# Splits, rotation tables and first block of the attention layer made beside the local stage

## What is computed

```python
x = x + layernorm(sparse_attention(layernorm(x)))    # compressed + selected + window branches, gated
x = x + layernorm(ffn_part(layernorm(x)))            # two layers of _layer below
```

```python
starts = np.arange(0, Lp - W + 1, W // 2)            # W = 64
win = xw[:, starts[:, None] + np.arange(W)]
win_out = attend(win, Wq, bq, Wk, bk, Wv, bv)        # softmax(q k^T * SCALE) v
out = concat([comp_out * g0, sel_out * g1, win_out * g2]) @ Wo + bo
out = out * 0.5 + hidden_states * 0.5
return (out - out.mean(-1)) * rsqrt(out.var(-1) + 1e-06)
```

```python
h = shift_token(x)                  # second half of the columns from the token before
q, k, v = split(h @ wqkv)
q = l2norm(q) * qs ; k = l2norm(k) * ksc
q, k = rotary_xpos(q, k)            # cos/sin tables times a scale by position
x = x + local_attention(q, k, v) @ wo
h = layernorm(shift_token(x)) * lg + lb
a, g = split(h @ w1 + b1)
x = x + (a * gelu(g)) @ w2 + b2
```

## Time and profile before

| | us |
|---|---|
| median of 3 runs (lowest, highest) | 1570.95 (1570.84, 1571.41) |
| the profiled execution's own time | 1571.91 |
| its span, first to last instruction | 1570.0 |
| TensorE / VectorE / ScalarE / GpSimd busy | 1468.3 / 1167.7 / 1033.9 / 779.5 |
| mean granted TensorE clock, share of 2.4 GHz | 0.972 |

### The profile page before, as it was taken

The page is one execution under the profiler, slowest core; times in us unless marked ns, Lnnn a source line. Parts: engine busy times, 40 slices in busy tenths (PEclk is TensorE's granted clock), DMA queues, the critical chain, the costliest instruction groups (busy, mean ns, idle before and its releaser), DMA issues.

```text
span 1570.0 us, 35727 instructions
## 1 busy us (share of the span) xinstructions
PE 1468.3 (94%) x10355; PEld 1214.9 (77%) x10355; DVE 1167.7 (74%) x3324; ACT 1033.9 (66%) x2610; POOL 779.5 (50%) x966
## 2 busy tenths in 40 slices
PE   8899992799999999988999979999999999799996
PEld 6468881688888888867888868888888887688885
DVE  6762686788888888876556568888888887666664
ACT  5222575588888888874545448888888888455553
POOL 4003245566666666633222536666666665344442
PEclk9999996899999999999999999999999999899998
DMA  5002233100000000002000020000000000000101
GB/s 179 1 1 69 95 101 90 55 7 6 6 5 5 5 5 5 5 8 83 14 13 9 14 65 5 7 6 5 5 5 5 5 5 6 31 28 28 53 28 54
DMA packets 57521, 44.04 MB, mean 28 GB/s; under 512 B 13214, under 2 KB 55386, under 8 KB 57442
## 3 DMA queue, kind: packets, MB, share of 16 engines
q1 hardware_dynamic: 57442, 43.07, 9.0%
HBM read 26.24 MB, written 8.39 MB: 22 GB/s over the span
## 4 chain that ended last, share of the span: by engine, by line
PE 80%; DVE 9%; ACT 4%; issue 4%; POOL 3%; DVEq 1%; ACTq 0%; DMA 0%; POOLq 0%; SPq 0%; PEldq 0%
PE bank L1948 7%; PE bank L1916 7%; PE bank L1862 7%; PE bank L1875 7%; PE bank L1781 6%; PE bank L1783 6%; PE bank L1782 6%; PE bank L1809 4%; PE bank L2019 4%; PE bank L2021 4%; PE bank L2020 4%; PE bank L1643 2%; PE bank L1703 2%; PE bank L1705 2%; PE bank L1704 2%
## 5 line engine op out<-in xcount | busy, mean ns | idle before, releaser
L1232 ACT ACTIVATE prob<-prob,neg_max 128x256 f32<-128x256 f32 x512 | 257.8, 507 | 9.2 <-DVE neg_max L2549 5.9
L798 POOL TENSOR_TENSOR rnorm<-sumsq,neg_half 128x8 f32<-128x8 f32 x128 | 213.0, 1664 | 23.4 <-POOL sumsq L795 23.4
L812 POOL TENSOR_TENSOR qk_cos<-qk_cos,qk_sin 128x512 f32<-128x512 f32 x128 | 181.1, 1415 | 60.7 <-DVE qk_cos L2413 44.9
L1781 PE MATMUL bank<-wqkv_hi,hT_hi 128*128 128x512 f32 x384 | 176.1, 458 | 4.9 <-DVE hT_lo L2399 4.9
L2019 PE MATMUL bank<-h_hi,w_hi 128*128 128x512 f32 (+1 forms) x352 | 143.7, 408 | 12.5 <-POOL h_lo L860 12.5
L1783 PE MATMUL bank<-wqkv_hi,hT_lo 128*128 128x512 f32 x384 | 154.8, 403 | 0.0
L1782 PE MATMUL bank<-wqkv_lo,hT_hi 128*128 128x512 f32 x384 | 153.9, 401 | 0.0
L1374 ACT ACTIVATE act_hi<-act_full 128x512 fp32r<-128x512 f32 x96 | 60.7, 632 | 138.9 <-DVE act_full L2735 137.4
L1916 PE MATMUL bank<-ident,prob 128*128 128x128 f32 x1024 | 147.1, 276 | 3.0 <-DVE prob L2588 2.1
L1916 PEld LDWEIGHTS bank<-ident,prob 128*128 128x128 f32 x1024 | 117.9, 141 | 30.4 <-DVE prob L2588 3.4
L2020 PE MATMUL bank<-h_hi,w_lo 128*128 128x512 f32 (+1 forms) x352 | 141.0, 401 | 0.0
(11 more groups left out here) (278 smaller groups left out, 4062.1 us busy)
## 6 DMA issues: line engine op xcount, KB each, us to landing
x_sb<-in_L_attn_hidden_states SPq DMA_DIRECT2D x8, 512.0 KB, 7.1
x_in<-in_L_attn_hidden_states SPq DMA_DIRECT2D x8, 512.0 KB, 4.8
x_scratch<-x_in SPq DMA_DIRECT2D x8, 512.0 KB, 3.0
f_x<-x_scratch SPq DMA_DIRECT2D x8, 512.0 KB, 4.1
out<-f_y SPq DMA_DIRECT2D x8, 512.0 KB, 3.0
raw<-in_L_ffn_w SPq DMA_DIRECT2D x6, 640.0 KB
hs<-x_sb SPq DMA_DIRECT2D x16, 224.0 KB
hs<-x_sb SPq DMA_DIRECT2D x64, 56.0 KB
```

The source lines that it names most:

```text
L798: pool.tensor_tensor(rnorm[:, part * HEADS:(part + 1) * HEADS], sumsq[:, which * HEADS:(which + 1) * HEADS], neg_half[:, 0:HEADS], ALU.pow ...
L812: pool.tensor_tensor(qk_cos[:, which], qk_cos[:, which], qk_sin[:, which], ALU.add).then_inc(z_ready[which], 1)
L1232: act.activation(prob[:, h], prob[:, h], ACT.Exp, bias=neg_max[:, h:h + 1], scale=-1.0, accum_out=psums[:, h:h + 1]).then_inc(exped, 1)
L1781: pe.matmul(bank[:, to], hT_hi[:, c], wqkv_hi[:, c, cols], start=(c == 0), stop=False)
```

## The change

The SBUF layout is made anew: rope, wqkv_hi, wqkv_lo, sc_x and wo_sb now start above everything that the local stage uses, while w1, w2, h_in and prob take the place of xnT and its weights; qTw and vw go over qT_lo and kT_lo. hT_hi and hT_lo still lie over the x_in ring (slot 0). The second and third rendezvous are gone. Work that stood between them is put into the local stage:

- ScalarE makes wqkv_hi in four halves (128x768) at the ends of its iterations n = 8, 11, 14, 17; VectorE wqkv_lo at the ends of its iterations 10, 13, 16, 19.
- GpSimd makes the scales after group step G = 1 and all eight tables, one at the end of each step G = 1 to 8.
- GpSimd stages block 0 at the start of G = 8; TensorE transposes it before its last window output; ScalarE makes hT_hi at n = 44, between `norm_x1` of group 6 and of group 7; VectorE makes hT_lo after its loop.
- `clear` comes after ScalarE's step 0 of layer 0.
- SP waits for the previous group's moves and store before issuing the next; GpSimd waits for the moves of groups 0 and 1, and after six steps for all.

```diff
+TABLES = 6 + 8
+SPLIT_AT = (8, 11, 14, 17)
+QKV_HALVES = (slice(0, 3 * INNER // 2), slice(3 * INNER // 2, 3 * INNER))
...
             def move_group(g):
                 sp.wait_ge(x_made, GB * (g + 1))
+                if g:
+                    sp.wait_ge(hs_moved, 48 * g)
+                    settle(sp)
...
-            await_phase(sp, 2)
             for lay in range(DEPTH):
-                if not lay:
-                    end_phase(sp, 3)
...
+            def stage_first():
+                pool.wait_ge(win_qk_ps, NB)
+                pool.wait_ge(hs_moved, 48)
+                settle(pool)
+                pool.tensor_copy(h_in[:, 0], x_sb[:, 0, 0:P]).then_inc(h_staged, 1)
+                pool.tensor_copy(h_in[:, 1], hs[:, 0, :]).then_inc(h_staged, 1)
             for G in range(1, NG + 3):
+                if G == NG:
+                    stage_first()
                 if 0 <= G - 2 < NG - LATE:
                     make_x1(G - 2)
                 if G - 1 < NG:
                     sum_scales(G - 1)
                 if 0 <= G - 3 < NG:
                     x1_scales(G - 3)
-            arrive(pool)
-            await_phase(pool, 2)
+                if G == 1:
+                    scales(0)
+                if G <= 8:
+                    table(*tables()[G - 1]).then_inc(sc_made, 1)
+            pool.wait_ge(hs_moved, 48 * 2)
...
+            def first_hi():
+                act.wait_ge(hT_ps, 1)
+                act.wait_ge(x1_stored, 16 * 5)
+                act.activation(hT_hi[:], bank[:, 3, 0:2 * P]..., ACT.Copy).then_inc(hT_hi_ready, 1)
...
+                if n == NB + 12:
+                    first_hi()
                 if r < 2 and 0 <= n - 16 < NB:
                     norm_x1(b)
                     norm_x1(b + 1)
-            end_phase(act, 2)
-            for c in range(DC):
-                act.activation(wqkv_hi[:, c], raw[:, c], ACT.Copy).then_inc(split_hi, 1)
+                if n in SPLIT_AT:
+                    c, h = divmod(SPLIT_AT.index(n), 2)
+                    act.wait_ge(raw_attn, 16)
+                    act.activation(wqkv_hi[:, c, QKV_HALVES[h]], raw[:, c, QKV_HALVES[h]], ACT.Copy).then_inc(split_hi, 1)
...
+                if n == NB - 1:
+                    first_turn()
                 win_out(n)
-            end_phase(pe, 2)
...
-            dve.wait_ge(x_made, NB)
-            await_phase(dve, 2)
+                lo(0, ahead=True)
+                if lay: ...
+                else:
+                    dve.wait_ge(x_made, NB)
+                    dve.wait_ge(x1_stored, 16 * NG)
```

More of the change, by code:

```diff
@@ L92, in build @@
         place("spare", [P, 2 * P])
+        sin_at = base[0]
+        sin_raw = place("sin_raw", [P, 2, BPB * 32])
         ident = place("ident", [P, P])
@@ L136, in build @@
         pT = place("pT", [P, 2, 4 * P])
-        oT = place("oT", [P, INNER // P, P])
         bst = place("bst", [P, GB, 2, 6])
@@ L204, in build @@
         pTw = place("pTw", [P, 2, P])
-        base[0] = after_const
+        base[0] = rope_at
+        wv_sb = place("wv_sb", [P, DC, D])
+        wc_sb = place("wc_sb", [P, RATIO * DC, D])
+        wo3_sb = place("wo3_sb", [P, 3 * DC, D])
+        wsg_sb = place("wsg_sb", [P, DC, 32])
+        bo_bc = place("bo_bc", [P, D])
+        iota1 = place("iota1", [P, P])
         l_bst = place("l_bst", [P, NB, 6])
@@ L921, in _ @@
                     scales(lay + 1)
-                    for a in range(2):
-                        for i in range(2):
-                            for h in range(2):
-                                table(a, i, h).then_inc(sc_made, 1)
+                    for which in tables():
+                        table(*which).then_inc(sc_made, 1)
                     pool.wait_ge(hs_moved, moved_in(lay + 1) - 48)
@@ L1124, in _ @@
                     act.wait_ge(x1_stored, 16 * NG)
-                    clear()
-                    end_phase(act, 3)
                 k0 = lay * NB
                 def hi(b):
+                    if not lay and type(b) is int and b == 0:
+                        return
                     act.wait_ge(hT_ps, k0 + b + 1)
@@ L1676, in win_out, with first_turn @@
                 pe.matmul(bank[:, 6 + j % 2, 0:D], pTw[0:WK, j % 2], vw[0:WK, j % 2], start=True, stop=True).then_inc(win_o, 1)
+            def first_turn():
+                pe.wait_ge(h_staged, 2)
+                pe.wait_ge(win_v, NB)
+                for c in range(DC):
+                    tr = pe.transpose(bank[:, 3, c * P:(c + 1) * P], h_in[:, c], ident[:])
+                tr.then_inc(hT_ps, 1)
             for k in range(5):
@@ L1708, in _ @@
             for lay in range(DEPTH):
-                if not lay:
-                    end_phase(pe, 3)
                 k0 = lay * NB
                 def transposes(b, ahead=False):
-                    if lay and type(b) is int and b == 0 and not ahead:
+                    if type(b) is int and b == 0 and not ahead:
                         return
```

177 lines of the change are left out of this document (84 added, 93 removed).

## The result

| | before | after |
|---|---|---|
| median of 4 runs (lowest, highest), us | 1571.18 (1570.84, 1574.56) | 1554.05 (1553.17, 1554.39) |
| ratio, 95% interval | | 0.9885 [0.987, 0.99] |
| profiled execution: span, us | 1570.0 | 1551.4 |
| mean granted TensorE clock | 0.972 | 0.977 |

The change gains 17.1 us where the prediction said 12.8: the time lies 0.75 us under the lower end of its range. The boundary is much as forecast; the surplus lies where the prediction had costed nothing.

What follows compares the result with a forecast made beforehand. TensorE, busy nearly throughout, idles before layer 0's first projection, on which everything later hangs. Starting it 15.5 us earlier, less 1.2, 1.25 and 0.3, gives 12.8 us: 1570.95 becomes 1558.2, range 1554.8 to 1561.5.

Steps and rivals of the forecast that it cites:

- What holds the first projection: Start of layer 0: hT_hi, behind group 6's norms, decides; without delays the projection starts at 256.55, 15.5 us earlier.
- (a): Turn of group 7: a table and block 0's staging delay VectorE's x_sb addition by 1.2 us (0.6 to 1.75).
- (b): End of the local stage: VectorE's last residual sum waits for GpSimd's last table, 1.25 us (0.7 to 1.25).
- (c): Local stage itself: the moved splits and the tables of steps 1 to 6 cost 0.3 us (0 to 3.0).
- The sum, 12.75: First projection and everything after it: 15.5 less 1.2, 1.25 and 0.3 us, so 12.8 us earlier.
- From the first projection on every block has its old length: All blocks after the first projection: durations unchanged, everything only moves earlier with it.
- I expect the same start at 1.2 GHz and cost nothing: Start of layer 0: TensorE's clock is low as before, costed at nothing; range ends 3.5 us gain, 1.5 us loss.
- Rival 2: After layer 0's start: the clock rises sooner, 3.5 us less, 1554.7; chance 0.13.
- The tables (1): Local stage: added tables and lo halves hold VectorE and reach TensorE, 1565.2, at worst 1571.7; chance 0.10.
- SP (3): Local stage's x_in ring: SP's waits for moves become the bound, kernel slower, 1579 if moves take 12 us; chance 0.02.
- The change does what it says (4): Layer 0's start: rival that the first projection still waits for the whole tail, gain 11, 1560.0; chance 0.05.

Runs made afterwards that it cites:

- e3: The changed kernel with GpSimd's eight rotation tables at group steps 1, 1, 2, 2, 3, 4, 5, 6, none at 7 and 8; median 1552.4 us.
- e6: The changed kernel with the hi and lo splits of the qkv weights moved back behind the loops of ScalarE and VectorE; median 1561.13 us.
- e1: The changed kernel run again, unaltered, against the kernel before; median 1553.89 us, ratio 0.99.
- e5: The changed kernel with one rendezvous put back between the local stage and layer 0; median 1557.29 us.
- e2: The kernel before with only the new SBUF layout, order of work and waits unaltered; median 1567.03 us, ratio to before 0.9979.
- e7: The changed kernel with 32 bytes left free ahead of the rotation tables and 32 more behind wo; median 1557.72 us.
- e4: The changed kernel with 26 idle matmuls of 256 columns on TensorE behind its last window output; median 1552.83 us.
- e13: The changed kernel with 32 bytes free ahead of the rotation tables, so qkv weights and work buffers start at 0 modulo 128; median 1550.4 us.

## Why the prediction was off, step by step

- **What holds the first projection: right.** The chain named (norms of group 6, hT_hi, hT_lo) is the one in the trace.
- **(a), 1.2: right in kind, 1.48 measured.** The x_sb addition went from 244.25 to 245.39, and the stage stood 0.34 earlier by then. The second copy waited behind the residual sum, the worse of the two orders between which I had taken the middle.
- **(b), 1.25: right in kind,** 2.19 - 1.22 = 0.97 measured. The table came first; the two overlapped by less than a whole table.
- **(c), 0.3:** 0.43, by one lo half. The moved tables cost the local stage nothing (e3, e6).
- **The sum, 12.75: right.** 12.54 measured, 12.63 again in e1. With the measured terms it is 15.5 - 1.48 - 0.97 - 0.43 = 12.62, and e3 gets 2.43 back without (a) and (b). That the sum hit so well is in part luck: (a) and (c) were too small by 0.4 together, (b) too large by 0.3. e5 and e6 priced what stood between: 2.2 and 5.7 us.
- **"From the first projection on every block has its old length": the step that failed.** I took a new layout for bookkeeping. It gave 0.29 + 1.28 + 0.52 + 0.47 = 2.6 us in the profiled pair, 2.3 in e2's trace and 2.9 between e7's and after's; the medians move by 3.3 (e2 alone) and 3.7 (e7, which takes it back, above after), and some of that may be clock. With the old starts the changed kernel takes 1557.72. That is half a microsecond from my 1558.2, but against the 1571.54 of before beside it the gain is 13.8 and not 12.8: the clock's share is still in it (1.49 us from the first projection to block 3).
- **"I expect the same start at 1.2 GHz and cost nothing": failed too.** Rival 2 came about: the clock had risen for good by 274 and not only by 292, worth 1.97 us to block 3, and missed its second fall in layer 1, worth 0.80. My ground against it was weak: the runs before lay within 0.6 us of each other, but they were three, and the thirteen beside e1 to e4 cover 1567.69 to 1573.18. Its price of 3.5 was an upper end. That its time of 1554.7 is close to the result is half chance: the other half of the surplus is the layout's.
- **The other rivals.** The tables (1) held VectorE only where (a) and (b) say. SP (3) had no share: the window outputs lose nothing but the 0.43 up to the last one. The change does what it says (4); e5, its likeness, is 1557.29.
- **The range** had room for one surprise on the low side, not for two.

## What to carry to other kernels

When buffers are laid out anew, the durations of the trace of before are no longer sure: in a kernel bound by TensorE allow some 0.5% either way (here padding alone gave 0.5% more and 0.3% less than the change as it was), and try a few pads of 32 bytes, each in front of what streams or is loaded into TensorE. Work that is moved in beside another stage is cheap where it meets idle engines, but place it away from the chain that ends the stage: two tables cost 2.4 us in steps 7 and 8 of GpSimd's loop and nothing measurable in steps 1 to 6. Leave room in a range for the clock as well: its rises and falls came at other places in kernels with the same addresses, worth 0.8 to 2 us each time. Two single traces are compared stretch by stretch, with the clock of each stretch beside it.

## What was not expected of the hardware

- **SBUF addresses change matmul times.** 128x512 matmuls with h_hi and w_hi took 404 to 409 ns on average by where h_hi starts (the lower mean of e13 is the clock's), those with w_lo 397 to 402 between two starts 128 bytes apart; 28 attention blocks 357.0 to 359.7 us; the whole kernel 1549.9 to 1561.97 with nothing but up to 160 bytes of padding. Why is open: neither "one good start" modulo 128 nor "distance" fits all rows, and the tables, wo and f_x1 were never moved apart from the qkv weights.
- **The clock falls in pauses of a few microseconds too**, not only in the long hole: from 1.00 to 0.50 within block 0 of the kernel after, where TensorE did nothing in 264 to 268. Keeping it busy there moved the fall to 276 to 280 in one kernel.
- **A copy with one SBUF input waited for a VectorE sum with two** (0.29 to 1.29 us), as VectorE waits for GpSimd.
